# Padding the variance product to 128 stationary columns, and moving a segment's last stores past a block boundary

## What is computed

```
xn    = layernorm(group_norm(x)) * g + b
left  = xn @ Wl.T * mask * sigmoid(xn @ Wlg.T)
right = xn @ Wr.T * mask * sigmoid(xn @ Wrg.T)
gate  = sigmoid(xn @ Wog.T)
out   = einsum('bikd,bjkd->bijd', left, right)
x     = x + (layernorm(out) * gate) @ Wout.T
```

## Time and profile before

| | us |
|---|---|
| median of 3 runs | 2158.09 |
| range of the runs | 2158.0 to 2159.71 |
| the profiled execution | 2161.47 |
| its span, first to last instruction | 2159.6 |

### The profile page before, as it was taken

The page is one execution under the profiler, slowest core; times in us unless marked ns, Lnnn a source line. Parts: engine busy times, 40 slices in busy tenths (PEclk is TensorE's granted clock), DMA queues, the critical chain, the costliest instruction groups (busy, mean ns, idle before and its releaser), DMA issues. The chain is left out here.

```text
span 2159.6 us, 40771 instructions
## 1 busy us (share of the span) xinstructions
PE 1792.7 (83%) x10305; PEld 966.5 (45%) x10389; DVE 1522.9 (71%) x3171; ACT 1310.5 (61%) x2413; POOL 808.0 (37%) x740
## 2 busy tenths in 40 slices
PE   0899996897998999965699799877799997699665
PEld 0234343785552343433355476633233333588332
DVE  7588887225754999996876487588488889344775
ACT  0577775466994777755599576433377776344322
POOL 0044445006980444445799100288000000000799
PEclk9999999898999999998899899999899999899999
DMA  7367777775994446446499686299447776754799
GB/s 316 118 190 224 241 217 219 292 311 175 362 369 137 137 156 194 156 147 234 152 366 360 228 293 225 95 396 398 151 149 222 236 231 207 266 232 161 246 354 333
DMA packets 336162, 512.88 MB, mean 237 GB/s; under 512 B 23979, under 2 KB 189486, under 8 KB 329654
## 3 DMA queue, kind: packets, MB, share of 16 engines
q1 hardware_dynamic: 336054, 511.65, 69.3%
HBM read 293.46 MB, written 205.52 MB: 231 GB/s over the span
## 5 line engine op out<-in xcount | busy, mean ns | idle before, releaser
L1289 POOL TENSOR_TENSOR shared<-O,out_rs 128x128 f32<-128x128 f32 (+1 forms) x128 | 94.9, 743 | 687.3 <-DVE out_rs L1196 686.1
L591 PE MATMUL ps<-w_heads,hi 64*128 64x256 f16 x3072 | 292.1, 273 | 36.3 <-DVE sig L742 25.2
L654 ACT ACTIVATE sig<-ps,largest 128x512 f32<-128x512 f32 x384 | 246.8, 692 | 51.3 <-PE ps L591 49.8
L1087 ACT ACTIVATE O<-ps 128x512 f32 (+1 forms) x144 | 151.9, 1055 | 183.5 <-PE ps L1008 183.5
L635 ACT ACTIVATE zs<-ps,shift 128x512 f32<-128x512 f32 x192 | 131.9, 687 | 213.0 <-PE ps L559 213.0
L1333 PE MATMUL ps<-ident,shared 128*128 128x128 f32 (+1 forms) x1024 | 163.3, 284 | 107.9 <-POOL shared L1289 107.8
L1333 PEld LDWEIGHTS ps<-ident,shared 128*128 128x128 f32 (+1 forms) x1024 | 114.3, 133 | 278.3 <-POOL shared L1289 194.2
L591 PEld LDWEIGHTS ps<-w_heads,hi 64*128 64x128 f16 x3072 | 154.1, 95 | 181.3 <-issue 65.8
L559 PE MATMUL ps<-xs,center 128*128 128x512 f32 x384 | 204.7, 615 | 13.6 <-issue 10.4
L591 PE MATMUL ps<-w_heads,lo 64*128 64x256 f16 x1536 | 213.0, 272 | 0.0
L742 DVE SCALAR_TENSOR_TENSOR sig<-ps,largest,sig 128x512 f32<-128x512 f32 x256 | 179.9, 743 | 46.1 <-ACT sig L654 44.5
(11 more groups left out here) (156 smaller groups left out, 3635.0 us busy)
## 6 DMA issues: line engine op xcount, KB each, us to landing
shared<-left_right SPq DMA_DIRECT2D x34, 2048.0 KB, 10.1
shared<-gate SPq DMA_DIRECT2D x256, 256.0 KB, 4.5
gate<-gates SPq DMA_DIRECT2D x96, 512.0 KB, 2.9
x_dram<-shared SPq DMA_DIRECT2D x192, 256.0 KB, 4.4
shared<-x_dram SPq DMA_DIRECT2D x192, 256.0 KB, 4.7
xs<-x_dram SPq DMA_DIRECT2D x64, 512.0 KB, 4.1
left_right<-stage SPq DMA_DIRECT2D x64, 448.0 KB, 5.8
left_right<-shared SPq DMA_DIRECT2D x64, 448.0 KB, 5.7
```

Source lines behind the costliest of these rows:

```text
L591: last = pe.matmul(PAIR[row][:, g, kb * S:kb * S + S], tokens[half, q % 8, at:at + P], k["w_heads"][half, part, :], start=(step == 0), sto ...
L654: act.activation(sig[:, slot, :].rearrange("p (c e) -> p c e", c=4), pair(row, 0), ACT.Sigmoid, scale=k["largest"][:, 0:1]).then_inc(c["si ...
L1087: act.activation(o_of(ch), ps[h % 4 // 2][:, h % 2, :].rearrange("p (b g i) -> p b g i", b=2, g=2), ACT.Copy).then_inc(c["o_copied"].sem, 1)
```

## The change

The constant `var_w` becomes wider, the window that the variance product takes from it is 128 columns instead of 16, and `VAR` is the whole bank instead of its first 16 partitions; 126 of the 128 stationary columns are zero in each chunk. ScalarE still reads 16 partitions. To make room, `gn_sums` lies in the memory of `gn_stats`. The last segment's four `store_first` are still issued by the projection's SyncE program; its eight `store_part` move to the start of the triangle's, which waits for them and then loads. The semaphore's counts follow.

```
-            "basis": sb("basis", [P, P]), "var_w": sb("var_w", [P, 4 * BATCH - 2]), "ident": sb("ident", [P, P]),
+            "basis": sb("basis", [P, P]), "var_w": sb("var_w", [P, 2 * BATCH - 2 + P]), "ident": sb("ident", [P, P]),
-            "gn": sb("gn", [P, 12]), "gn_stats": sb("gn_stats", [P, NCH, 6]), "gn_sums": sb("gn_sums", [P, 2, NCH]),
+            "gn": sb("gn", [P, 12]), "gn_stats": sb("gn_stats", [P, NCH, 6]),
+        k["gn_sums"] = k["gn_stats"][:].rearrange("p a b -> p (a b)")[:, 0:2 * NCH].rearrange("p (a n) -> p a n", a=2)
...
+def last_stage(blocks, low, groups):
+
+    second = blocks[:, 0, 1] if low == BF16 else blocks[:, :, 1].rearrange("p l b s e -> p (l b) s e")
+    return second.rearrange("p b s e -> p (b s e)").rearrange("p (g b l n e) -> p g b l n e", g=2, b=2, l=2, n=groups)
...
-        Z, VAR, R, GATE = ps[0][:, 0, :], ps[0][0:2 * BATCH, 1, :], ps[1][:, 0, :], ps[1][:, 1, :]
+        Z, VAR, R, GATE = ps[0][:, 0, :], ps[0][:, 1, :], ps[1][:, 0, :], ps[1][:, 1, :]
...
-            for q in range(SEG_PARTS // 2):
-                store_parts(bodies, q)
+            sp.wait_ge(c["lr_done"].sem, c["lr_done"](NCH * 2))
+            for lr in range(2):
+                for g in range(2):
+                    store_first(sp, blocks, stage[1], S // SEG // 2 - 1, lr, g, c["first_out1"])
...
-                w = k["var_w"][:, 2 * (BATCH - 1 - at):2 * (2 * BATCH - 1 - at)]
+                w = k["var_w"][:, 2 * (BATCH - 1 - at):2 * (BATCH - 1 - at) + P]
                 pe.matmul(VAR, w, sq[:, q % 2, :], start=(at == 0), stop=(at == BATCH - 1)).then_inc(c["var_done"].sem, 1)
...
-                act.activation(log_var[:], VAR, ACT.Ln, bias=k["unit"][0:2 * BATCH, 2:3]).then_inc(c["log_done"].sem, 1)
+                act.activation(log_var[:], VAR[0:2 * BATCH, :], ACT.Ln, bias=k["unit"][0:2 * BATCH, 2:3]).then_inc(c["log_done"].sem, 1)
...
-        c[f"lr_out{s}"].advance(128 * bodies)
+        c[f"lr_out{s}"].advance(16 * SEG_PARTS * (bodies - s))
...
-                sp.wait_ge(c["lr_out1"].sem, c["lr_out1"](0))
+                for part in range(SEG_PARTS):
+                    store_part(sp, left_right, last_stage(blocks, low, C // HG), S // SEG // 2 - 1, part, c["lr_out1"])
+                sp.wait_ge(c["lr_out1"].sem, c["lr_out1"](16 * SEG_PARTS))
                 load(0, 1)
```

More of the change, by code:

```diff
@@ L457, in project @@
         stage0 = sb("stage0", [P, 2, 2, 2, C // HG, SEG * HG], low)
-        second = blocks[:, 0, 1] if paired else blocks[:, :, 1].rearrange("p l b s e -> p (l b) s e")
-        stage = [stage0[:], second.rearrange("p b s e -> p (b s e)").rearrange("p (g b l n e) -> p g b l n e", g=2, b=2, l=2, n=C // HG)]
-        Z, VAR, R, GATE = ps[0][:, 0, :], ps[0][0:2 * BATCH, 1, :], ps[1][:, 0, :], ps[1][:, 1, :]
+        stage = [stage0[:], last_stage(blocks, low, C // HG)]
+        Z, VAR, R, GATE = ps[0][:, 0, :], ps[0][:, 1, :], ps[1][:, 0, :], ps[1][:, 1, :]
         PAIR = [ps[2], ps[3]]
@@ L1090, in triangle @@
     if not stays:
+        c["lr_out1"].advance(16 * SEG_PARTS)
         for s in range(2):
@@ L1431, in constants @@
     group = np.arange(P) % C // 2
-    var_w = np.zeros((P, 4 * BATCH - 2), np.float32)
+    var_w = np.zeros((P, 2 * BATCH - 2 + P), np.float32)
     spread = np.zeros((P, BATCH, P), np.float32)
```

## The result

| | before | after |
|---|---|---|
| median, us | 2158.52 (4 runs) | 2139.06 (4 runs, 2137.34 to 2139.81) |
| the profiled execution, us | 2161.47 | 2139.81 |
| its span, us | 2159.6 | 2137.9 |
| ratio of after to before | | 0.9906, 95% interval 0.989 to 0.9921 |

The kernel became faster by 0.94%, 19.5 us in the medians and 21.7 in the two profiled spans; 2137 was forecast, in a range of 2126 to 2150. Some lines are renumbered: variance product 578 (was 570), centring 567 (559), spread 586 (578), heads 599 (591), gate 606 to 608 (598 to 600), low part 736 (728), masks 799 (791), parts' stores 426 (425), first stores 439 (432), load 980 (972), pack 1042 (1032), contraction 1018 (1008), copy of O 1097 (1087).

What follows compares the result with a forecast made beforehand. TensorE was taken to bound the projections, already at 2.4 GHz, with VectorE nearly as late in layer 1. 2161.5 - 29.0 (columns) + 8.2 (stores) = 2140.7, less 3.4 for the median: 2137, range 2126 to 2150 (8 in 10).

Steps and rivals of the forecast that it cites:

- The gap around the variance product: TensorE in a projection step: 0.08 us saved ahead of the product, 0.01 between halves, 0.10 behind, 0.19 in sum.
- Rival (c): Variance product: its 128-column fp32 load is not pulled ahead, +0.12 us a product, kernel slower at 2189; 5%.
- (d): Variance product: gaps are tied to the loads' waits, so the columns gain nothing, 2166; 5%.
- How many steps pass it on: Projection steps shortened by 0.19 us: 42 of 48 in layer 0 (8.0 us), 36 in layer 3 (6.8 us).
- the step with the split: Layer 1, VectorE's step splitting r: 6.6 us without waiting for ScalarE, so eight chunks need at least 35.1.
- Part 1: Variance product in the projections, 128 columns for 16: 29.0 us saved, bounds 20 and 34.
- Rival (a): Projections: other engines, VectorE above all, take most of the columns' gain, leaving 15 us, total 2151; 15%.
- Part 2: Eight stores moved to the triangle's start: costs 8.2 us (layer 0 +5.0, layer 3 +2.2, layer 1 +1.0), bounds 2 and 13.
- lateness of the load: Layer 0's triangle: the second half's load waits for the later stores, so that half starts 2.4 us later.
- restart at the lower clock: Layer 0's triangle: TensorE comes out of ten idle us at 1.2 GHz, costing 2.6 us.
- Rival (b): Triangle starts: the load is not late and the moved stores gain 20 us, total 2109; 5%.
- The base: Whole kernel: profiled execution 2161.5 us, median 3.4 below it, so 2140.7 forecast for the execution becomes 2137 for the median.

Runs made afterwards that it cites:

- the stores alone: Changed kernel with the variance product back at 16 columns, the eight stores still moved: 2167.15 us, ratio 1.0029 to the kernel before.
- the columns alone: Kernel before with 128 stationary columns in the variance product, the eight stores left in the projection: 2134.46 us, ratio 0.9873 to the kernel before.
- the pairs with equal columns: Two comparisons of stores moved against not moved: at 16 columns (ratios to before 1.0029 and 1) and at 128 columns (0.9906 and 0.9873).
- the overlap run: Changed kernel with five of the eight stores back in the projection, reordered, each side's load waiting only for its own stores: 2124.8 us, ratio 0.9844 to before.

## Why the prediction was right, point by point

**The gap around the variance product.** -0.08 ahead was -0.09, -0.11 on halves and behind together was -0.11 (0.97 to 0.86), the step -0.21 where 4.31 less 0.19 was forecast (4.12, is 4.10). The cause, the change of shape, is shown by 64 and 72 columns. Rival (c), the load that is not pulled ahead, and (d) are out by the load's row at 186.12.

**How many steps pass it on.** Between centring products eight steps apart layer 0 went from 36.0 to 34.6 and layer 3 from 36.2 to 35.0, that is 7 and 6 steps of 0.2, as argued from the earlier trace rows. First to last centring product: layer 0 -10.5 for 10.9 forecast; layer 3 -11.0 for 9.7, of which -1.1 is the earlier return of TensorE's granted clock at the start of its projection; the stores alone show the same 1.1, the columns alone none. Why the stretch ahead runs differently was not looked for. Agreement to better than 1 us is luck: with the columns only layer 0 gains 11.5, and with the stores only, which change nothing ahead of that place, 0.9.

**Layer 1** was mis-sized: 8.4 forecast, 6.4 found (-7.2 to the last centring product, +0.8 from there to the end). The term was that of the step with the split, 6.6, my reading less a wait; it is 819.90 - 813.09 = 6.81, and 7 x 4.08 + 6.81 = 35.4. A slip adds 0.3: by the prediction's own terms the six batches give 6 x (36.02 - 35.16) = 5.2, not 5.5. That VectorE's side and not TensorE bounds the layer is shown by halving the subtraction; I had not seen that GpSimd's product is part of the ring.

Part 1 as a whole: 29.0 forecast, 27.9 by the spans of columns only. Rival (a), other engines absorbing half, is out. Its own 2151 lies outside the range that is said to take in most of it.

**Part 2 in layer 0.** +5.0 forecast, +4.9 found. Its two terms: lateness of the load 2.4, found 2.9 (+31.1 for +28.2; the stores start 2.1 later, and the load follows 15.5 after the first of them for 14.7, the slowest landing in 7.5 us for 6.3); restart at the lower clock 2.6, found 2.05 (1.7 to 2.7 over the kernels that have it). One too small and one too large: that the sum came out to 0.1 is luck, the more so as the last copies scatter by 2 us. VectorE's new idle stretch was 17.4 us for about 10, because it has packed its eight channels before TensorE has used them; TensorE's was 11.5. Why the slowest store lands 1.2 later is open.

**Part 2 in the other layers.** Layer 3: +2.2 forecast, +1.1 found. The load is issued 1.8 later (+17.2 for +15.4) but lands faster, in 12.9 us for 13.5, as this answer on line 980 for layer 3 shows:

```profile
DMA to landing us min/median/max: 8.4/10.6/12.9
```

Layer 1: +1.0 forecast, +1.6 found, and +2.0 or +2.7 in the pairs with equal columns. The second group is only 0.5 later (+22.6 for +22.1), so more than half of the shift was covered, as argued. But that slack is not a fixed one: in the pairs with equal columns the second group is 0.9 and 1.6 later (+23.0 for +22.1, +22.6 for +20.9). The rest comes behind it in the triangle and is not explained. Sum of the three +7.6 for 8.2; the runs with equal columns give 6.3 and 7.1 us. Rival (b), that the load is not late, would need all that the overlap run had to be built for.

**The base.** The spans differ by 21.7 (20.8 forecast), the medians by 19.5, since the profiled execution of before lay 3 us above its median and that of after 0.8 above its own; a part of what 2137 missed of 2139.06 is this.

## What to carry to other kernels

A small fp32 product between full ones on TensorE paid for its shape twice here, ahead (0.31 us for 0.22) and behind (0.97 for 0.86), and zero columns that make it full cost nothing while its longer load hides; look whether the load starts before its own product. Moving work behind a boundary lets another engine start earlier, but it gains only if what that engine needs next is not queued behind the same boundary: follow the queue to the next wait, and put the overlap there. Measure the parts alone: the sum of a good and a bad half still looks like a success.

## What was not expected of the hardware

A stationary operand of 64 columns is worse than one of 16: the step takes 4.35 us for 4.31, by its open load, and one of 72 costs as much as 128. VectorE's subtraction from SBUF to SBUF went on until 0.56 us (512 columns) or 0.28 us (256) behind the end of the GpSimd product beside it, having begun 1.0 us before that end in both; with GpSimd idle the one of 512 takes 0.69. GpSimd's product written to one bfloat16 element in sixteen took 2.33 us for 512 elements, where 1024 in neighbouring pairs took 2.04 and 512 in fp32 1.08.
